# x1 tiles split into halves by rows and turned into the activations' columns by DMA transposes, in place of TensorE transposes

## The reference

```
x1 = x  + L0_ffn(einsum('bct,bcd->bdt', x, L0_cond_weights[cond]))   # main = y @ W0.T, plus a gated LoRA
x2 = x1 + L1_ffn(L1_cond(x1))
L1_cond(x)  = einsum('bsi,boi->bso', x, L1_cond_weight[adapter_ids])  # 1024 x 1024 weight per batch
L1_ffn(h)   = bitlinear(bitlinear(h, w_gate) * bitlinear(h, w_up), w_down)
```

## Time and profile before

| | |
|---|---|
| median of 3 runs | 1480.62 us |
| lowest, highest run | 1472.19, 1484.09 us |
| the profiled execution's own time | 1473.58 us |
| its span, first to last instruction | 1471.9 us |
| TensorE busy | 1354.1 us, 92% |
| VectorE, ScalarE, GpSimd busy | 768.4, 356.5, 237.4 us |
| granted TensorE clock, mean | 0.972 |
| layer 0 over tiles 0 to 15 | to 336.6 us of the span |
| first product of layer 1 | 340.9 us |

### The profile page before, as it was taken

The page is one execution under the profiler, slowest core; times in us unless marked ns, Lnnn a source line. Parts: engine busy times, 40 slices in busy tenths (PEclk is TensorE's granted clock), DMA queues, the critical chain, the costliest instruction groups (busy, mean ns, idle before and its releaser), DMA issues.

```text
span 1471.9 us, 24964 instructions
## 1 busy us (share of the span) xinstructions
PE 1354.1 (92%) x8870; PEld 860.3 (58%) x8871; DVE 768.4 (52%) x1058; ACT 356.5 (24%) x393; POOL 237.4 (16%) x134
## 2 busy tenths in 40 slices
PE   4787998998999979778779999999999999999998
PEld 4784444444445444344334478884588864788843
DVE  5458555321554426877874535557155564355521
ACT  3331343000111235565552001111011110011100
POOL 3200000000000012334333002220022220022200
PEclk9898999999999988999999999999999999999999
DMA  8983799669997418787776454435544444544354
GB/s 216 292 254 101 272 411 394 217 187 279 276 269 231 130 47 294 261 276 265 255 230 250 158 208 150 150 140 215 205 181 150 150 175 158 208 150 150 140 214 136
DMA packets 174493, 310.63 MB, mean 211 GB/s; under 512 B 99520, under 2 KB 131520, under 8 KB 166624
## 3 DMA queue, kind: packets, MB, share of 16 engines
q1 hardware_dynamic: 159232, 254.23, 52.6%
q10 hardware_dynamic: 14176, 55.06, 9.9%
q0 software_dynamic: 1024, 0.53, 0.2%
HBM read 220.78 MB, written 68.03 MB: 196 GB/s over the span
## 4 chain that ended last, share of the span: by engine, by line
PE 63%; DVE 11%; DMA 9%; issue 7%; ACT 5%; SPq 3%; POOL 1%; ACTq 0%; POOLq 0%; DVEq 0%
PE pair L948 25%; PE pair L985 14%; PE pair L809 12%; PE pair L744 6%; DVE region_q L1609 3%; DMA region_q<-wb_scratch 2%; ACT region_q L1163 2%; DMA region_q<-in_L_cond_weight 2%; PE pair L653 2%; DVE region_q L1617 2%; DMA region_q<-in_x 2%; ACT region_w L1187 1%; PE pair L708 1%; PE pair L751 1%; DVE region_q L1620 1%
## 5 line engine op out<-in xcount | busy, mean ns | idle before, releaser
L948 PE MATMUL pair<-act_t,region_q 128*128 128x256 f16 x3696 | 404.0, 273 | 0.0
L948 PEld LDWEIGHTS pair<-act_t,region_q 128*128 128x128 f16 x3696 | 361.7, 98 | 42.5
L985 PE MATMUL pair<-region_q,region_w 128*128 128x512 f16 x1232 | 267.6, 379 | 6.8 <-DMA region_q<-wb_scratch 6.4
L632 POOL TENSOR_TENSOR region_w<-region_q,region_w 128x1792 f32 (+1 forms) x44 | 157.8, 3587 | 540.3 <-ACT region_w L1187 540.3
L985 PEld LDWEIGHTS pair<-region_q,region_w 128*128 128x128 f16 x1232 | 120.0, 98 | 153.3 <-DMA region_q<-wb_scratch 8.6
L809 PE MATMUL pair<-region_w,act_t 128*128 x816 | 181.3, 383 | 5.5 <-DMA region_w<-w1s_scratch 4.3
L744 PE MATMUL pair<-region_w,act_t 128*128 128x512 f16 x768 | 172.1, 381 | 0.0
L912 PE MATMUL pair<-act_t,region_q 128*128 128x512 f16 x704 | 165.6, 396 | 0.0
L809 PEld LDWEIGHTS pair<-region_w,act_t 128*128 x816 | 80.4, 99 | 100.2 <-issue 9.1
L1300 DVE SCALAR_TENSOR_TENSOR act_t<-pair,act_t 128x512 f32 (+2 forms) x66 | 61.1, 947 | 127.9 <-ACT act_t L1018 127.9
L744 PEld LDWEIGHTS pair<-region_w,act_t 128*128 (+1 forms) x768 | 75.5, 98 | 88.3 <-issue 1.9
(11 more groups left out here) (182 smaller groups left out, 1123.0 us busy)
## 6 DMA issues: line engine op xcount, KB each, us to landing
region_q<-wa_scratch SPq DMA_DIRECT2D x33, 1792.0 KB, 7.3
region_q<-wb_scratch SPq DMA_DIRECT2D x28, 1408.0 KB, 6.1
region_q<-in_L_cond_weight SPq DMA_DIRECT2D x40, 512.0 KB, 8.7
w1s_scratch<-region_q ACTq DMA_DIRECT2D x40, 512.0 KB, 8.2
wa_scratch<-region_q SPq DMA_DIRECT2D x22, 896.0 KB, 4.0
region_q<-in_x SPq DMA_DIRECT2D x64, 256.0 KB, 6.2
region_w<-in_L_ffn_w_gate SPq DMA_DIRECT2D x16, 688.0 KB, 9.9
wb_scratch<-region_q SPq DMA_DIRECT2D x11, 896.0 KB, 5.1
```

What stands on the lines that cost most here:

```text
L632: pool.tensor_tensor(at(iop[:, 1], u), st[s][:, 0:7], at(iop[:, 0], u), ALU.subtract)\
L948: mm = pe.matmul(bank(s_bank, b)[:, (1 - h) * HALF:(2 - h) * HALF], ring_a[s][:, h, o_a, k], moving[a], start=(opens and h == 1 and k == 0 ...
L985: mm = pe.matmul(bank(s_bank, b), iop[:, a, p, o_a, tp * P:(tp + 1) * P], ring_b[r][:, p], start=(opens and p == 0 and a == 0), stop=(not ...
```

## The change

TensorE's `turn_x1` and its semaphore go. ScalarE and VectorE now split x1 by rows, from `x1_nat[s]` into two pairs of fp16 tiles (`x1_high16`, `x1_low16`, 2 KB per partition each, in space that is free during layer 0). SP then moves each half into `act_t` by a DMA transpose (128 x 1024 fp16, 256 KB). In the loop it does so for tile t - 2, behind the x pair of tile t; the last two tiles are turned behind the loop. `x1_turned[s]` counts 16 per transpose: ScalarE waits for it before it writes the fp16 tiles again, and TensorE, ScalarE and VectorE wait for it at the start of layer 1. `load_rank(0)` and its waits are as before.

```diff
--- before.py
+++ after.py
@@ -125,6 +125,8 @@
         x_nat = [view(region_q, 32 + 4 * i, [D], F32) for i in range(2)]
         x1_nat = [view(region_q, 40 + 4 * i, [D], F32) for i in range(2)]
         mix_nat = [x_nat[0], x_nat[1], view(region_q, 48, [D], F32), view(region_q, 52, [D], F32)]
+        x1_high16 = [view(region_q, 56, [D], F16), view(region_q, 64, [D], F16)]
+        x1_low16 = [view(region_q, 58, [D], F16), view(region_w, 69.5, [D], F16)]
         gw1_nat = x1_nat[0]
         tmpw_t = view(region_q, 48, [2, NTOK], F16)
         lora_a_nat = view(region_q, 56, [KC, E, R], F32)
@@ -255,7 +257,7 @@
         tmpw_low = sem("tmpw_low")
         acc_released = sem("acc_released")
         main_done = sem("main_done")
-        x1_transposed = sem("x1_transposed")
+        x1_turned = [sem(f"x1_turned{i}") for i in range(2)]
         x1_high = sem("x1_high")
         x1_low = sem("x1_low")
         x1_stored = [sem(f"x1_stored{i}") for i in range(2)]
@@ -468,6 +470,11 @@
                 sp.wait_ge(y_done, NT)
                 load_pair(x_nat[t], x_loaded[t], t)
             sp.wait_ge(w_low, NPREP0 + KC)
+            def turn_x1(t, s):
+                sp.wait_ge(x1_low, t + 1)
+                for a, src in ((0, x1_high16[s]), (1, x1_low16[s])):
+                    sp.dma_start_transpose(act_t[:, a, :, ds(t * P, P)], src).then_inc(x1_turned[s], 16)
+
             def layer0(i, pieces):
                 for s in range(2):
                     t = 2 * i + s
@@ -478,6 +485,7 @@
                             load_w(w1_rows[ds(row_i + (4 * s + q) * P, P), :], NPREP0 + 4 * t + q, q)
                     sp.wait_ge(acc_released, t - 1)
                     load_pair(x_nat[s], x_loaded[s], t)
+                    turn_x1(t - 2, s)
                     if pieces:
                         load_gate(t, s)
 
@@ -485,6 +493,8 @@
                 layer0(i, False)
             with sp.Fori(NT // 4, NT // 2) as i:
                 layer0(i, True)
+            for s in range(2):
+                turn_x1(NT - 2 + s, s)
 
 
             def load_rank(r):
@@ -752,12 +762,6 @@
                                        lb[:, b, h * H:(h + 1) * H], start=False, stop=(a == 1))
                 mm.then_inc(main_done, 1)
 
-            def turn_x1(t, s):
-                pe.wait_ge(acc_released, t + 1)
-                wait_if(pe, x1_low, t)
-                transpose8(pair[2], x1_nat[s], ident).then_inc(x1_transposed, 1)
-
-
             pe.wait_ge(y_low, NT)
             for t in range(2):
                 for q in range(4):
@@ -777,13 +781,11 @@
             pe.wait_ge(tmpw_low, 2)
             lora(0, 0)
             lora(1, 1)
-            turn_x1(0, 0)
 
             def layer0(i):
                 for s in range(2):
                     t = 2 * i + s
                     main(t, s, 0)
-                    turn_x1(t - 1, 1 - s)
                     for q in range(1, 4):
                         main(t, s, q)
                     lora(t, s)
@@ -796,7 +798,8 @@
                 rank = field(pe, F_RANK, k, NADP - 1)
                 at = field(pe, F_READ, k, NB * SEQ)
                 if isinstance(k, int) and k == 0:
-                    pe.wait_ge(x1_low, 2)
+                    pe.wait_ge(x1_turned[0], 32)
+                    pe.wait_ge(x1_turned[1], 32)
                     pe.wait_ge(acc_released, NT)
                 pe.wait_ge(w1_loaded, rank * 32 + 32)
                 wait_if(pe, z_copied_a, k - 1)
@@ -815,7 +818,10 @@
             def linear_t(k, s):
                 pe.wait_ge(z_copied_a, k + 1)
                 pe.wait_ge(z_copied_v, k + 1)
-                pe.wait_ge(x1_low, NT) if isinstance(k, int) and k == 0 else wait_if(pe, z_low, k)
+                if isinstance(k, int) and k == 0:
+                    pe.wait_ge(x1_turned[0], 16 * NT)
+                    pe.wait_ge(x1_turned[1], 16 * NT)
+                wait_if(pe, z_low, k)
                 transpose8(pair[2], z_nat[s], ident).then_inc(z_transposed, 1)
 
             pe.wait_ge(consts_ready, 9)
@@ -827,10 +833,8 @@
 
 
             linear(0, 0)
-            turn_x1(NT - 1, 1)
             linear(1, 1)
             linear_t(0, 0)
-            pe.wait_ge(x1_low, NT)
             linear(2, 0)
             linear_t(1, 1)
             with loop(pe, 1, NSLOT // 2 - 4) as i:
@@ -1083,8 +1087,10 @@
                 high(tmpw_t[:, 0, i * D:(i + 1) * D], pair[2 + i][:, :], 1.0).then_inc(tmpw_high, 1)
 
             def x1_part(t, s):
-                act.wait_ge(x1_transposed, t + 1)
-                high(act_t[:, 0, :, ds(t * P, P)], ps8[2], ACT_SCALE).then_inc(x1_high, 1)
+                act.wait_ge(acc_released, t + 1)
+                if not isinstance(t, int) or t >= 2:
+                    act.wait_ge(x1_turned[s], 16 * t - 16 * s)
+                high(x1_high16[s], x1_nat[s], ACT_SCALE).then_inc(x1_high, 1)
                 act.dma_start(x1_dram[ds(t * P, P), :], x1_nat[s]).then_inc(x1_stored[s], 16)
 
             def layer0(i):
@@ -1135,6 +1141,8 @@
                 with act.If(used > r):
                     for s in range(4):
                         act.wait_ge(w_stored[s], stores(2 * r + 2, s))
+            for s in range(2):
+                act.wait_ge(x1_turned[s], 16 * NT)
             load_piece(0, 0)
             load_piece(1, 1)
             copy_z(0, 0)
@@ -1516,18 +1524,17 @@
                 v.scalar_tensor_tensor(out=x1_nat[s], in0=pair[s][:, :], scalar=1.0 / PROD, in1=x_nat[s],
                                        op0=ALU.mult, op1=ALU.add).then_inc(acc_released, 1)
 
-            def low_x1(t):
+            def low_x1(t, s):
                 v.wait_ge(x1_high, t + 1)
-                low(act_t[:, 1, :, ds(t * P, P)], ps8[2], ACT_SCALE, act_t[:, 0, :, ds(t * P, P)])\
-                    .then_inc(x1_low, 1)
+                low(x1_low16[s], x1_nat[s], ACT_SCALE, x1_high16[s]).then_inc(x1_low, 1)
 
             residual(0, 0)
             residual(1, 1)
-            low_x1(0)
+            low_x1(0, 0)
             def layer0(i, pieces):
                 for s in range(2):
                     t = 2 * i + s
-                    low_x1(t - 1)
+                    low_x1(t - 1, 1 - s)
                     used = field(v, F_USED, 0, NADP)
                     with v.If(used > i):
                         for q in range(4):
@@ -1540,7 +1547,7 @@
                 layer0(i, False)
             with v.Fori(NT // 4, NT // 2) as i:
                 layer0(i, True)
-            low_x1(NT - 1)
+            low_x1(NT - 1, 1)
             v.wait_ge(gate_summed, NPIECE_G)
             v.tensor_reduce(ssum[:, 0:1], stat_g[:, :], X, ALU.add).then_inc(stat_summed, 1)
 
@@ -1571,6 +1578,8 @@
                 low_z(2 * i + 1)
                 sum_piece(2 * i + 1, 1, 32 * i + 32, last)
 
+            for s in range(2):
+                v.wait_ge(x1_turned[s], 16 * NT)
             copy_z(0, 0)
             with v.Fori(0, NPIECE // 2 - 1) as i:
                 layer1(i)
```

## The result

| | before | after |
|---|---|---|
| median | 1479.82 us (4 runs, 1472.19 to 1484.09) | 1529.48 us (4 runs, 1525.86 to 1532.78) |
| profiled execution, its span | 1473.58, 1471.9 us | 1532.78, 1531.1 us |
| TensorE busy | 1354.1 us, 92% | 1351.1 us, 88% |
| granted TensorE clock, mean | 0.972 | 0.949 |

The changed kernel is slower: ratio 1.0341, 95% interval 1.0292 to 1.039. The medians differ by 49.7 us, the two profiled executions by 59.2. Some executions of several kernels here, the one before included, take 1.5 to 5% longer than the rest (two of its 16 runs beside the last experiments lay at 1508.69 and 1526.02 us); the ratios leave them out, the medians given do not.

The account below looks back on a forecast made before the run. TensorE carries 63% of the chain, with full DMA engines and rank 0's load nearly as late. +12.7 - 5.2 - 0.9 + 28.6 = +35.2 on 1473.6 gives 1508.8; 7.0 more for the median, 1515.8 us; range 1492 to 1550.

Parts of the forecast that it names:

- R2: Rival: turns read from SBUF cost up to 4.1 us or somewhat over; sum +53, 1534 us; chance 0.15.
- (a): TensorE: sixteen transpose groups go, fifteen in layer 0, one in layer 1; 13.9 us if all on the path.
- tiles 10 to 15 well over 11.66: Sign in layer 0 that the forecast is wrong: these tiles slower would mean turns dearer than their bytes.
- nothing is gained in the full tiles: Layer 0, full DMA stretch: the 9 x 0.87 us taken off TensorE gain nothing, since TensorE only waits longer.
- (b): Layer 0, SP's queue: two DMA transposes per tile; seven turns in full traffic add 12.7 us, later ones are hidden.
- I take 1.8, by bytes: Layer 0: a tile's two transposes take 1.8 us of all DMA engines, at the w1 transposes' 290 GB/s.
- R3: Rival: each turn instruction holds SP like a w1 transpose, 7.43 us at least; sum +101, 1582 us; chance 0.07.
- comparison by blocks: Under R3: the skill's 1309 ns per 128x128 block by DMA set against 80 ns each in a 2 MB stream.
- (c): End of layer 0: SP issues rank 0 behind the last turns, so layer 1 starts 32.9 us behind, not 4.3; +28.6.
- The 6.2 us to the issue: From layer 0's last product: residual, split of the last tile and SP's two turn issues before rank 0's load.
- The lower end of 16.5: Rank 0's load at its cheapest: 4.2 MB at 290 GB/s and 2 us of start; 26.4 us was taken.

Follow-up runs that it names:

- the last experiments: DMA turns only for tiles 9 to 15, rank 0 behind tile 11, ScalarE's pieces later, against the kernel before: 1479.79 us beside 1474.17, ratio 1.0044.
- the DMA-only kernel: No reference work, only DMA transposes and copies, zeros stored; four 256 KB transposes beside plain stores took 16.27 us from SBUF, 12.71 from DRAM.

## Why the prediction was right, and where its terms were off

The forecast was 1515.8 us, the result 1529.48; it lies inside the range 1492 to 1550 and at the upper end of the forecast's own 1500 to 1530. The direction and the two places of the loss held: full DMA engines in layer 0, and the late rank load. On the profiled execution the sum was 24 us short, both large terms too small and nothing cancelling; that the result is inside the range is owed to the range's width, which R2's price had set, more than to the sum.

- **(a) and the tiles behind the full stretch.** Right for tiles 12 to 15, at 11.66 us. Tiles 10 and 11 took 17.2 and 13.3 us, and tiles 2 to 9 16.0 us on average against the 13.5 to 14.5 forecast; the sign "tiles 10 to 15 well over 11.66", set down for turns dearer than their bytes, came true in part. The step that nothing is gained in the full tiles held for the sum, not for its course: TensorE was 4.9 us ahead at tile 6 and then gave it back in stalls.
- **(b), layer 0: mis-sized.** Predicted +12.7 - 5.2 = +7.5, measured +20.3. The step that failed is "I take 1.8, by bytes". Alone, a turn takes 2.8 us, since 290 GB/s holds for transposes of 2 MB and those of 256 KB run at 188. From tile 1's turn at 168 us to tile 8's at 290 there are eight turns in full traffic, not seven (before, the full stretch lasts to 270 us and not 262: the share is 1.00 from 260 to 270 and 0.36 from 270 to 280); 8 x 2.8 = 22.4, close to the +23.8 at tile 12. That agreement isn't proof: with half the bytes tile 12 came 2 to 6 us earlier and not 12, and the median stayed. What the runs show is that a turn holds SP for some 9 us in full traffic, that this hold is half of the chain there, and that the engines move 316 GB/s in place of 408 meanwhile. A second term is missing from the sum, the slow products behind each stall: as seen from TensorE the +23.8 are 31.5 us of stalls and 9.4 of slow products, less the 7.2 of the stall before and eleven groups of 0.87 (24.1, an estimate from these figures). How the stalls divide between the transposes' own time on the engines and the held queue stays open. One lead was not followed: from 150 to 310 us either kernel moves 50 MB, the changed one in 33,438 DMA packets, 22,624 of them under 512 bytes, the kernel before in 13,603, with 1,696 under 512.
- **R3, dear per instruction.** Named for a turn that holds SP 7.43 us an instruction. Its condition was met in the full stretch, in part (9 us per turn, not 15), and its price was not: it took the hold to be the same in quiet tiles, where it is 2.88 us, and one instruction in place of two did not lower the time. In its comparison by blocks a number is wrong: 2 MB of fp16 are 64 blocks of 128x128, not 128, so they land at 160 ns each and not 80. A turn's blocks, 1.37 us for eight, take 171 ns each, nearly the same.
- **R2, dear per byte.** Part of it was right: 2.8 us is between 1.8 and 4.1. Its reason, the source in SBUF, was wrong; alone, DRAM costs the same.
- **(c), the order on SP: right, and the largest term.** Predicted +28.6, measured +37.0. The 6.2 us to the issue were 6.5. The load and the start behind it were put at 26.7 us and took 34.85: that is the mis-sized part. The lower end of 16.5 is near what it takes alone (18.5 and 17.9), and the four pieces make up the rest. I had named them and then priced them by a load that had other company.
- **Pieces not foreseen.** That holding the pieces back only moves the collision to rank 1.

**Predicted and measured in one line:** +35.2 on the profiled execution, of which 7.5 layer 0, 28.6 pause, -0.9 layer 1; measured +59.2, of which 20.3, 37.0 and 1.9 (a gap of 1.12 us and a slow first product group at the start of layer 1). The medians are only 49.7 apart: the profiled execution of the kernel before lay 6.2 us under its median, that of the changed one 3.3 over.

The Trainium skill, "Advanced Engine Details and Errata", section "X-Bar Transpose (TRN2)", puts transposing DMAs at the rate of regular ones, 350 to 400 GB/s. The runs differ: 188 GB/s at 256 KB, 271 at 2 MB, 382 for plain copies in the same kernel.

## What to carry to other kernels

Before work is moved from an engine to a DMA queue, look at the queue's order and not only at its bytes: what the new instruction stands in front of, and what it must wait for, was the larger part here (16 us for a single load issued late, 37 with company). A DMA transpose belongs in a stretch in which the DMA engines have room; in a full one a turn of 512 KB held its queue for 7 to 14 us here and a load of 4 MB for up to 50, and all that is queued behind it, while TensorE's eight transposes cost 0.87 us. A stall costs more than its length, as the products behind it run slowly at first. When a collision between transfers is removed by delaying one, look for the next transfer that it will meet.

## What the runs showed of the hardware

- DMA transposes of 256 KB ran at 188 to 189 GB/s from SBUF and DRAM alike, one of 2 MB at 271, plain copies at 382.
- A DMA transpose beside plain transfers of other queues holds its issuing queue for longer. For 256 KB: 1.3 us alone and up to 7.4 beside stores in the DMA-only kernel; 1.27 us in quiet tiles of layer 0, and in full traffic between 200 and 290 us 7.4 to 9.9 where a turn is one such transpose, 1.27 to 9.47 each where it is two. For 2 MB: 7.43 to 11.6 in layer 1 before, and 8.8 and 40.9 in the full stretch.
- The 48 products of a tile took 10.52 us at a granted clock of 1.00, and 11.93 to 13.28 behind five stalls of 3.2 to 14.6 us, during the longest of which the clock fell to 0.50.
